# A fused attention and feed-forward block: norm of the fourth block moved to VectorE, output tiles in other banks, a store on another queue, new engine orders

## What is computed

```python
x = x + layernorm(attention(layernorm(x), W_qkv))      # one head of width 128
z = layernorm(x)
h = silu(z @ w1.T * s1) * (z @ w2.T * s2)              # 128 -> 512, gated
h = gelu(h @ h1.T * sh1)                               # 512 -> 512
h = gelu(h @ h2.T * sh2)                               # 512 -> 512
x = x + layernorm(h @ w3.T * s3)                       # 512 -> 128
```

## Time and profile before

| | us |
|---|---|
| median of 3 runs | 134.03 |
| lowest and highest | 133.97 and 134.73 |
| the profiled execution | 134.5 |
| its span, first to last instruction | 132.6 |
| TensorE busy in the span | 125.5 |
| VectorE busy | 104.7 |
| ScalarE busy | 98.5 |
| GpSimd busy | 28.3 |

### The profile page before, as it was taken

One profiled execution on the slowest core, in us unless ns is written; L12 is line 12 of the kernel. 1 busy time (PEld: TensorE's weight loads), 2 busy tenths in 40 slices (PEclk: granted clock), 3 DMA queues, 4 the chain that ended last, 5 costly groups with the idle time before them and its releaser, 6 DMA issues. The chain is left out here.

```text
span 132.6 us, 2374 instructions
## 1 busy us (share of the span) xinstructions
PE 125.5 (95%) x699; PEld 103.3 (78%) x699; DVE 104.7 (79%) x356; ACT 98.5 (74%) x184; POOL 28.3 (21%) x39
## 2 busy tenths in 40 slices
PE   6999998999989999999999999999999999999970
PEld 4685968889876888887889888888776788789960
DVE  1769599999899998938799999566989973996433
ACT  3128779878799919389999277799991996996640
POOL 4281330034210013400200174300002530000352
PEclk9999999999999999999999999999999999999996
DMA  4899997000200000000000001020000002000002
GB/s 112 262 278 405 374 374 240 0 0 5 82 0 5 0 5 2 0 0 0 5 0 0 0 5 40 2 79 7 0 0 0 0 0 84 0 5 0 2 29 94
DMA packets 5344, 8.28 MB, mean 62 GB/s; under 512 B 464, under 2 KB 2768, under 8 KB 5328
## 3 DMA queue, kind: packets, MB, share of 16 engines
q1 hardware_dynamic: 3984, 5.19, 12.3%
q0 software_dynamic: 1344, 2.88, 6.6%
HBM read 7.02 MB, written 1.05 MB: 61 GB/s over the span
## 5 line engine op out<-in xcount | busy, mean ns | idle before, releaser
L317 POOL TENSOR_TENSOR rstd<-ve,minus_half 128x4 f32<-128x4 f32 (+1 forms) x19 | 18.5, 974 | 92.7 <-DVE ve L678 51.6
L1147 PE MATMUL F<-a_hi,h_hi 128*128 128x512 f32 (+1 forms) x160 | 37.7, 357 | 0.0
L1153 PE MATMUL F<-a_lo,h_hi 128*128 128x512 f32 (+1 forms) x160 | 37.3, 353 | 0.1
L610 DVE TENSOR_TENSOR a_lo<-act_full,a_hi 128x512 fp32r<-128x512 f32 (+1 forms) x52 | 30.0, 604 | 3.7 <-ACT act_full L427 3.2
L435 ACT ACTIVATE a_hi<-F,sc 128x512 fp32r<-128x512 f32 (+1 forms) x35 | 21.1, 625 | 14.6 <-PE F L1153 14.5
L1153 PEld LDWEIGHTS F<-a_lo,h_hi 128*128 128x128 f32 x160 | 26.8, 188 | 5.4 <-DVE a_lo L610 1.1
L1147 PEld LDWEIGHTS F<-a_hi,h_hi 128*128 128x128 f32 x160 | 26.0, 188 | 4.5 <-DVE a_hi L716 0.6
L427 ACT ACTIVATE act_full<-F,sc 128x512 f32<-128x512 f32 (+1 forms) x40 | 23.3, 619 | 1.0 <-PE F L1153 1.0
L708 DVE SCALAR_TENSOR_TENSOR act_full<-F,sc,silu 128x512 f32<-128x512 f32 (+1 forms) x16 | 10.7, 681 | 1.7 <-ACT silu L416 1.4
L1104 PE MATMUL F<-x2T_hi,w_hi 128*128 128x512 f32 (+1 forms) x32 | 10.3, 404 | 0.5 <-DVE x2T_lo L610 0.3
L416 ACT ACTIVATE silu<-F,sc 128x512 f32<-128x512 f32 (+1 forms) x16 | 9.8, 634 | 0.9 <-PE F L1107 0.7
(11 more groups left out here) (154 smaller groups left out, 197.5 us busy)
## 6 DMA issues: line engine op xcount, KB each, us to landing
h_raw<-h SPq DMA_DIRECT2D x2, 1024.0 KB, 11.4
h_hi<-h POOLq DMA_DIRECT2D x2, 1024.0 KB, 8.7
xs<-x SPq DMA_DIRECT2D x3, 256.0 KB, 3.7
out<-outs SPq DMA_DIRECT2D x3, 256.0 KB, 2.2
w_raw<-w SPq DMA_DIRECT2D x1, 512.0 KB, 6.6
w_hi<-w POOLq DMA_DIRECT2D x1, 512.0 KB, 7.4
xs<-x SPq DMA_DIRECT2D x2, 128.0 KB, 7.8
w_raw<-w SPq DMA_DIRECT2D x1, 256.0 KB, 15.1
```

Source lines behind the costliest of these rows:

```text
L317: nc.gpsimd.tensor_tensor(rstd[:, ln, tiles(b)], ve[:, ln, tiles(b)], minus_half[:, 0:SIZES[b]], ALU.pow).then_inc(rstd_ready[ln], 1)
L610: nc.vector.tensor_tensor(dst, full, hi.bitcast(f32), ALU.subtract).then_inc(done, 1)
L1147: nc.tensor.matmul(out, terms[k][0], terms[k][2], start=(k == 0), stop=False)
L1153: last = [nc.tensor.matmul(out, terms[k][0], terms[k][3], start=False, stop=(k == KT - 1)) for out, terms in groups]
```

## The change

- `y_normalised(3)` goes from ScalarE to VectorE, right behind `y_shifts(3)`; `last_add(3)` waits for it by a semaphore of its own.
- `last_bank(t)` is F[t] in place of A[2], A[1]: the last tiles' products wait for the last block's gelus, no longer for the fourth block's norm. The eight `last_down` come in another order.
- `store_last(1)` is issued by ScalarE, and `store_last(0)` by SyncE as before.
- `LOW_PARTS` puts w1 and w2 alone in the first group and all else in the second. The first hidden layer's branch asks the second flag, so that `low_sum(5)`, `copy_flags(1)` and `read_flag(1)` come before the end of `A1` of block 0.
- Nine of the twenty high parts of A1 are copied by ScalarE (`HIGH_ON_ACT`). `pT_copy(1, 0)`, `pT_copy(2, 0)` and `gT_copy(3)` go to ScalarE, `xT_copy(2)` and `gT_copy(2)` to VectorE.
- GpSimd issues the rounding loads of w1, w2, h1 and h2 behind its first root. TensorE has one more warm-up product before the first transposes.
- The lists of ScalarE, VectorE, GpSimd and TensorE are rearranged, through all five blocks. `GELU_ONCE` says what `CAST_SLICES` said, and `gated` gives the same buffer.

The diff, cut to the definitions, the orders of the first two blocks and the last, and some of VectorE's between:

```diff
@@ -80,7 +80,7 @@
         ones_sq, w3_diag, w3_row = sb("ones_sq", [P, P]), sb("w3_diag", [P, D]), sb("w3_row", [P, D])
         w3_scaled = sb("w3_scaled", [P, KT * D])
         flags = sb("flags", [1, 2])
-        LOW_PARTS = ((0, 3), (3, 6))
+        LOW_PARTS = ((0, 1), (1, 6))
@@ -182,12 +182,14 @@
-        third_cast = sem("third_layer_cast")
+        a1_hi_by_act = sem("a1_hi_by_act")
+        a_cast = [None] + [sem(f"a{n}_cast") for n in (2, 3)]
...
-        y_shift_ready, yn_ready, out_ready, last_ready, out_stored = (
-            sem("y_shift_ready"), sem("yn_ready"), sem("out_ready"), sem("last_ready"), sem("out_stored"))
+        y_shift_ready, yn_ready, yn_by_dve, out_ready, last_ready, out_stored = (
+            sem("y_shift_ready"), sem("yn_ready"), sem("yn_by_dve"), sem("out_ready"), sem("last_ready"), sem("out_stored"))
+        last_stored = sem("last_stored")
@@ -198,14 +200,19 @@
-        CAST_SLICES = 1
+        HIGH_ON_ACT = (1, 1, 0, 0, 0, 1, 1, 1, 0, 0, 0, 1, 0, 0, 1, 1, 0, 0, 0, 1)
+
+        GELU_ONCE = ((), (12,))
 
         def hi_done(n, b, o):
-            if n < A3 or b < LAST - 1:
-                return a_hi_ready[n], KT * b + o + 1
-            if o < CAST_SLICES:
-                return third_cast, o + 1
-            return a_hi_ready[A3], KT * b + o + 1 - CAST_SLICES
+            i = KT * b + o
+            if n == A1:
+                on_act = HIGH_ON_ACT[i]
+                return (a_hi_ready[A1], a1_hi_by_act)[on_act], sum(e == on_act for e in HIGH_ON_ACT[0:i + 1])
+            by_cast = GELU_ONCE[n - 1]
+            if i in by_cast:
+                return a_cast[n], by_cast.index(i) + 1
+            return a_hi_ready[n], i + 1 - sum(k < i for k in by_cast)
@@ -221,7 +228,7 @@
-        BY_DVE = ((0, 0, 0, 1, 1), (0, 0, 0, 1, 1), (0, 0, 0, 1, 1), (1, 1, 0, 1, 1, 1, 0, 1))
+        BY_DVE = ((0, 0, 1, 1, 1), (0, 0, 1, 0, 1), (0, 0, 0, 1, 1), (1, 0, 0, 0, 1, 1, 0, 1))
@@ -245,7 +252,7 @@
-            return (A[2], A[1], A[3], A[0])[t]
+            return F[t]
@@ -285,8 +292,8 @@
-            store_last(1)
-            sp.wait_ge(out_stored, 16 * (LAST + SIZES[LAST]))
+            sp.wait_ge(out_stored, 16 * (LAST + SIZES[LAST] - 1))
+            sp.wait_ge(last_stored, 16)
@@ -331,29 +338,32 @@
-                pool.wait_ge(yn_ready, T0[b + 1])
+                if b == LAST - 1:
+                    pool.wait_ge(yn_by_dve, SIZES[b])
+                else:
+                    pool.wait_ge(yn_ready, T0[b + 1])
...
             rsqrt(LN_X, 0)
+            round_w12()
+            round_h1()
+            round_h2()
             rsqrt(LN_X, 1)
-            round_w12()
             rsqrt(LN_X, 2)
-            round_h1()
             rsqrt(LN_O, 0)
-            round_h2()
             rsqrt(LN_X1, 0)
+            round_w3()
             rsqrt(LN_O, 1)
             rsqrt(LN_X1, 1)
-            round_w3()
             rsqrt(LN_X, 3)
             rsqrt(LN_O, 2)
             rsqrt(LN_Y, 0)
+            rsqrt(LN_X, 4)
             rsqrt(LN_X1, 2)
-            rsqrt(LN_X, 4)
+            last_add(0)
+            rsqrt(LN_Y, 1)
             rsqrt(LN_O, 3)
-            rsqrt(LN_Y, 1)
-            last_add(0)
@@ -416,6 +426,13 @@
+            def high(n, b, o):
+                c = slice(0, width(b))
+                if b > 0:
+                    act.wait_ge(*a_used(n, b))
+                act.wait_ge(a_full[n], KT * b + o + 1)
+                nc.scalar.activation(a_hi[n][:, o, c], full_of(n, b)[:, o, c], ACT.Copy).then_inc(a1_hi_by_act, 1)
...
+            def store_last(t):
+                g, j = G0[LAST] + t // 2, t % 2
+                act.wait_ge(last_ready, t + 1)
+                nc.scalar.dma_start(out_view[:, g, j * D:(j + 1) * D], outs[:, T0[LAST] + t, :]).then_inc(last_stored, 16)
@@ -467,23 +489,24 @@
             qk_copy()
             xT_copy(0)
             gT_copy(0)
+            exps(0, 0)
             v_copy(0)
-            exps(0, 0)
             xT_copy(1)
             low_sum(0)
             gT_copy(1)
-            xT_copy(2)
             low_sum(1)
+            v_copy(1)
             exps(1, 0)
-            v_copy(1)
-            gT_copy(2)
+            v_copy(2)
             exps(1, 1)
             x2T_high(0)
             silu(0, 0)
+            pT_copy(1, 0)
             silu(0, 1)
-            v_copy(2)
+            pT_copy(1, 1)
+            high(A1, 0, 0)
             silu(0, 2)
-            pT_copy(1, 1)
+            high(A1, 0, 1)
             silu(0, 3)
             exps(2, 0)
             gelu_high(A2, 0, 0)
@@ -491,39 +514,44 @@
             gelu(A2, 0, 0)
             gelu(A2, 0, 1)
             gelu_high(A2, 0, 2)
+            gelu(A2, 0, 2)
             gelu_high(A2, 0, 3)
-            gelu(A2, 0, 2)
             gelu(A2, 0, 3)
+            exps(2, 1)
             gelu_high(A3, 0, 0)
+            x2T_high(1)
+            gelu_high(A3, 0, 1)
             gelu(A3, 0, 0)
-            gelu_high(A3, 0, 1)
+            gelu_high(A3, 0, 2)
             gelu(A3, 0, 1)
-            x2T_high(1)
-            gelu_high(A3, 0, 2)
+            gelu(A3, 0, 2)
+            pT_copy(2, 0)
             gelu_high(A3, 0, 3)
-            gelu(A3, 0, 2)
             gelu(A3, 0, 3)
             silu(1, 0)
             silu(1, 1)
-            exps(2, 1)
             silu(1, 2)
             silu(1, 3)
+            high(A1, 1, 1)
+            high(A1, 1, 2)
             scaled_yT(0)
+            high(A1, 1, 3)
             gelu_high(A2, 1, 0)
@@ -591,9 +623,9 @@
             gelu(A2, 4, 3)
             gelu(A3, 4, 0)
             gelu(A3, 4, 1)
-            y_normalised(3)
             gelu(A3, 4, 2)
             gelu(A3, 4, 3)
+            store_last(1)
...
+            def y_normalised(b):
+                dve.wait_ge(y_shift_ready, b + 1)
+                dve.wait_ge(out_ready, b)
+                for t in range(SIZES[b]):
+                    n = T0[b] + t
+                    nc.vector.tensor_scalar(y_n[:, t, :], A[2][:, t * D:(t + 1) * D], rstd[:, LN_Y, n:n + 1], y_shift[:, n:n + 1],
+                                            ALU.mult, ALU.add).then_inc(yn_by_dve, 1)
@@ -795,35 +835,35 @@
             squared_sums(0)
             w3_row_copy()
             pT_copy(0, 0)
+            xT_copy(2)
             attention_out(0)
             maxima(1, 0)
             x1_block(0)
             maxima(1, 1)
+            copy_flags(0)
+            x1_normalised(0)
             low_sum(2)
-            x1_normalised(0)
-            pT_copy(1, 0)
-            squared_sums(1)
-            copy_flags(0)
+            gT_copy(2)
             x2T_low(0)
             low_sum(3)
             low_sum(4)
             gate(0, 0)
+            low_sum(5)
             gate(0, 1)
-            high(A1, 0, 0)
-            high(A1, 0, 1)
-            low_sum(5)
+            maxima(2, 0)
             low(A1, 0, 0)
             gate(0, 2)
             low(A1, 0, 1)
             high(A1, 0, 2)
-            maxima(2, 0)
+            gate(0, 3)
             low(A1, 0, 2)
+            high(A1, 0, 3)
+            copy_flags(1)
+            squared_sums(1)
+            low(A1, 0, 3)
             attention_out(1)
-            gate(0, 3)
-            copy_flags(1)
-            high(A1, 0, 3)
-            low(A1, 0, 3)
             x1_block(1)
+            maxima(2, 1)
             low(A2, 0, 0)
             low(A2, 0, 1)
             low(A2, 0, 2)
@@ -832,128 +872,119 @@
             x_statistics(3)
             x2T_low(1)
             low(A3, 0, 0)
+            squared_sums(2)
+            x_statistics(4)
+            low(A3, 0, 1)
+            low(A3, 0, 2)
             x_normalised(3)
-            pT_copy(2, 0)
-            maxima(2, 1)
-            low(A3, 0, 1)
+            pT_copy(2, 1)
+            low(A3, 0, 3)
             gate(1, 0)
             gate(1, 1)
             high(A1, 1, 0)
-            high(A1, 1, 1)
-            low(A3, 0, 2)
+            xT_copy(3)
             low(A1, 1, 0)
-            low(A3, 0, 3)
-            pT_copy(2, 1)
+            gate(1, 2)
             low(A1, 1, 1)
-            gate(1, 2)
             gate(1, 3)
-            high(A1, 1, 2)
-            squared_sums(2)
-            high(A1, 1, 3)
             low(A1, 1, 2)
+            attention_out(2)
             low(A1, 1, 3)
-            attention_out(2)
             y_statistics(0)
+            y_shifts(0)
             x1_block(2)
             low(A2, 1, 0)
             low(A2, 1, 1)
             low(A2, 1, 2)
             low(A2, 1, 3)
-            xT_copy(3)
             x1_normalised(2)
-            y_shifts(0)
+            low(A3, 1, 0)
             x2T_low(2)
-            low(A3, 1, 0)
...
+            low(A1, 2, 2)
             gate(2, 3)
-            low(A1, 2, 2)
-            squared_sums(3)
-            high(A1, 2, 3)
+            y_statistics(1)
+            low(A1, 2, 3)
             attention_out(3)
-            low(A1, 2, 3)
-            y_statistics(1)
+            low(A2, 2, 0)
             x1_block(3)
```

(54 more changed lines are left out.)

101 lines of the change are left out of this document (50 added, 51 removed).

## The result

The changed kernel takes 135.47 us (median of 10 runs, 134.79 to 136.25) beside 134.01 for the kernel before (10 runs, 133.46 to 134.73): a ratio of 1.0096, 95% interval [1.0066, 1.0126]. It is 1.3 to 1.5 us slower, where 0.26 less was forecast. The profiled execution took 136.25 us with a span of 134.4, against 134.5 and 132.6 before. Executions more than 1.5 per cent above the fastest of their kernel are left out of all ratios; the traces of e1 and e11 are of such executions.

What follows compares the result with a forecast made beforehand. VectorE and ScalarE were taken to bound the kernel up to about 45 us, TensorE after. Terms of +0.19 to the last products and -0.45 for the tail gave -0.26: 133.8 us from 134.03, 8 in 10 within 132.4 to 135.5.

Steps and rivals of the forecast that it cites:

- blocks 1 to 3, +0.45: Up to 89 us: VectorE waits for two roots, TensorE's products in hand cover nearly all; +0.45 us, between 0 and 1.95.
- The flag: Last weight sum, flag copy and flag read come some 5 us earlier on VectorE, still ready in time; 0.
- The loads, 0: GpSimd's earlier rounding loads cost 0 if the raw h1 weights slip by less than 1.6 us, as assumed.
- The second hidden layer of block 0, +1.16: VectorE idles for GpSimd's root before x1_block(1), so A2's low parts come late; +1.16 us, between 0 and 1.4.
- The stalls at 36.94 and 40.51: TensorE's waits before block 0's later transposes and block 1's A1 go; terms -0.31 and -0.36 us.
- the whole first stretch: First x1 transposes of block 0 to its first y transposes; terms behind the first up give +0.24 us.
- 96 to 112 us, -0.65: Blocks 3 and 4: high parts on ScalarE relieve VectorE, evening TensorE's starts; -0.65 us, between 0 and -0.7.
- The tail, -0.45: From the last products on: norm on VectorE, earlier last gelu, separate store queues; -0.45 us, between -0.1 and -0.6.
- The warm-up, +0.10: A seventh warm-up product on TensorE before the first transposes; +0.10 us, between 0 and +0.21.
- The rival in which the roots reach TensorE: VectorE's waits for GpSimd's roots delay TensorE in every block, no relief at 96 to 112 us; 135.9 us, chance 0.16.
- the three signs that were to show the forecast wrong: ScalarE idle at its second weight sum; second-layer TensorE stall over 0.5 us from block 1; table switch above 1.3.
- the drain: Rival: ScalarE's table switch costs 2.66 us with a 1380 ns drain, delaying x2T_high(1) by 2.8; 136.0 us, chance 0.02.

Runs made afterwards that it cites:

- e1: The changed kernel with GpSimd's rounding loads back at their old places: 135.16 us, 1.0077 of the kernel before.
- e11: e5 with low_sum(5) reading the long-landed raw h2 weights instead of w3, so no wait for w3: 134.22 us, 0.9995 of the kernel before.
- e5: The changed kernel with GpSimd's last_add(0) and last_add(1) waiting until VectorE has written the normalised x1 two blocks on: 134.37 us, 1.0005 of the kernel before.
- e6: e5 with GpSimd's rounding loads also back at their old places: 134.02 us, 0.9990 of the kernel before.
- e10: e6 with squared_sums(1) and attention_out(1) earlier on VectorE, and x1_block(2) ahead of y_shifts(0): 134.86 us, 1.0049 of the kernel before.
- e2: The changed kernel, loads still early, with low_sum(5) moved behind low(A1, 0, 0) on VectorE: 135.19 us, 1.0092 of the kernel before.
- e4: The kernel before with only the tail of the change: 134.01 us, 0.9999 of the kernel before.
- e12: e6 with the tail of the kernel before: 134.34 us, 1.0023 of the kernel before.
- e8: The kernel before with y_shifts(1) moved ahead of xT_copy(4) and low(A2, 2, 2), so an add meets VectorE's norm: 134.65 us, 1.0038 of the kernel before.
- e3: The kernel before with only GpSimd's loads moved early as in the change: 133.80 us, 0.9996 of the kernel before.

## Why the prediction was wrong

**The step that failed most: blocks 1 to 3, +0.45.** It went through VectorE's waits for roots and asked whether TensorE's products in hand cover them. What it left out is that moving `y_shifts` moves three things: the shifts on VectorE, the norm on ScalarE, and the add on GpSimd, and that the last one's cost depends on what VectorE does at that moment. The forecast took VectorE's four instructions at 1.11 us wherever they stand. They measured 1.54 and 2.12; 0.92 us reached TensorE in the trace, and the time fell by 0.91 per cent, 1.2 us with 0.6 of uncertainty, when the adds were held back (e5 against the kernel after). The row that could have warned was in the trace of before: the add ran behind the norm, at 85.20 behind 84.6, by half a microsecond.

Without the collision this stretch costs +0.83 (e6), inside the range of 0 to 1.95 but nearly twice the 0.45. It was not the first root: e10 takes VectorE's wait for it away, and TensorE's stretch stays at 9.0. In e6 one low part of block 1's second layer starts 0.29 later than even, at 49.39; the rest was not traced to a cause.

**The flag, "VectorE had them done ... and now still has", priced at 0.** The place of the sum was checked against TensorE's need, not against the landing of its own data. In the trace this costs 1.14 us (16.59 against 15.45). In the time it is small: 0.19 per cent from e1, 0.15 from e6 against e5, 0.10 from e11, each with an uncertainty of 0.4 to 0.5. Where it didn't wait, the sum came 3.5 to 3.7 us behind the first x1 transposes in the kernels with its new place (e2 apart), and w3 landed between 22.40 and 23.66 in the five traces with early loads. An execution whose transposes start at 20 would hardly wait (20 + 3.6 against 23.66 at the latest); the profiled ones of the kernel after and e5 started at 18.9 and 18.1 and paid it whole.

That most executions simply begin late is unlikely. From the first x1 transposes to the end the trace of e11 takes 113.48 us, and the spans of its eleven shorter executions are 131.5 to 132.7, which puts their transposes at 18.0 to 19.2, an estimate that holds if the part behind them repeats as it does in the traces. The same working gives medians of 18.6 to 19.1 for e1 to e4 and e6 to e12, but 18.2 for the kernel after and 17.9 for e5, the two that were traced with the wait. If these begin like the others, they paid not the whole 1.14 but between 0 and 0.7 of it. Then w3 must land earlier in most executions than in the traces; no trace shows that, and the reason stays open.

**The loads, 0.** The forecast took the raw h1 weights to slip by less than 1.6 us. They slipped by 2.1 (12.39 to 14.53), and ScalarE idled for 0.53. That the term is 0 all the same is luck: ScalarE's next wait, for TensorE, hid it.

**The second hidden layer of block 0, +1.16,** was right in its mechanism: idle of 1.16 for the root, the lows late. Its size was too big: TensorE's low products start 1.14 later than even (1.19 in e6), where 1.6 was forecast; beside the 0.4 that the forecast had for before, this is about +0.75. The stalls at 36.94 and 40.51 are gone, as forecast. Without the wait for w3 the whole first stretch is -0.15 against +0.24 forecast (e6).

**96 to 112 us, -0.65,** was mis-sized. The pair of products that started 0.56 apart in the earlier trace rows does start 0.47 apart after the change, but from y of block 2 to the x1 transposes of block 4 all that is gained is 0.27: 7.97 us instead of 8.24. Of this 0.16 (0.23 in e6) is lost again before the last products. Part of that may be the same as above: GpSimd's third add, beside subtractions with two inputs in memory, takes 1725 ns instead of 1300, and the subtraction at its end 887 instead of 683.

**The tail, -0.45,** measured -0.44 in the trace, with its steps: the last gelu ends 0.67 us behind the start of the last products instead of 1.13, these take 1.95 us instead of 2.12, the last stores are 0.27 apart (less than 0.2 was expected). In the time it can't be told from 0.

**The warm-up, +0.10, and the part ahead of the first x1 transposes** can't be checked: this landmark scatters by more than a microsecond from one trace to the next.

**Rivals and signs.** The rival in which the roots reach TensorE gave 135.9, near the measured 135.5, and 135.5 is also the slow end of the range given for 8 in 10. Both are luck: the time was close and the mechanism was another. Of the three signs that were to show the forecast wrong, one came: ScalarE idles at its second weight sum. It is not what made the kernel slower. No second layer from block 1 on has a stall above 0.5 (the largest is 0.29), and a table switch still takes 1.30 us from its load to the next activation (27.01 to 28.30 in e6), so the drain stays out. The loss sat in the transposes, which the list of signs did not watch.

Summed up: with both unforeseen losses out, the kernel (e6) takes 0.999 of the time before, 133.9 us where 133.77 was forecast; the two make the other 1.4. How near 133.9 is to 133.77 says little, at 0.4 of uncertainty. In the traces e6 is 0.20 us longer than before from the first x1 transposes to the end (113.47 against 113.27), where the terms of this part were to give -0.41: too little gained at 96 to 112 us and too much lost in blocks 1 to 3, in part made up by the second hidden layer.

## What to carry to other kernels

When a step moves, follow every instruction that it releases to its own engine, and for each add on GpSimd ask which instruction of VectorE runs at that time; an add on an engine that has time to spare can hold another engine for nearly the add's own length. Check a moved reader against its writer too: the time at which its data arrive, and how that time and its turn scatter. Where two engines are both full, judge a place in one list by what the other engine waits for, not only by TensorE.

## What the runs showed of the hardware

**GpSimd's add holds up VectorE's norm.** A norm instruction (tensor_scalar, 128x128) of 341 ns that starts just behind the start of an add takes 768 or 1347 ns and ends 90 ns behind it, at 58.05 and 85.69 in the kernel after, and 1320 ns in e8, 84 ns behind it; the length follows the add's end, which looks like a block for the rest of the add and not like a slower rate. The Trainium skill, "SBUF — State Buffer", section "Who interferes with whom", says that the two engines share one pair of ports, which VectorE uses in its 2-port modes, that whoever comes first holds it for its whole instruction, and that the other stands still. The traces agree. Not each instruction suffers: in the kernel before, BATCH_NORM_STATS2 keeps its 276 ns beside the add at 79.07; in e5 the copy from a bank at 85.63, beside the add, took 426 ns, its usual length. By the same section a copy or tensor_scalar can enter these modes, and a tensor_tensor with both inputs in SBUF contends with a GpSimd instruction that reads SBUF, which fits the add of 1725 ns.

**A load's landing depends on another queue's issues.** With GpSimd's first three rounding loads issued 3 to 10 us earlier (4.61, 5.35 and 6.11 in the kernel after, 7.93, 9.70 and 16.14 before) and its last at 18.44 instead of 32.86, SyncE's w3 load landed at 22.4 to 23.7 us in five executions; with them at their old places, at 18.8 to 21.8 in nine. It was issued between 5 and 6.5 us in both. Which part of sharing the DMA engines delays it was not tested.

**The beginning scatters more than the rest.** The first x1 transposes start at 18.1 to 20.0 us in twelve of the fourteen traces and at 20.2 and 20.5 in the other two, although the kernels are nearly the same up to there, while the stretch from there to the last products repeats to within 0.3 us (before, e3, e4: 107.03, 107.02, 107.27; e6, e12: 107.67, 107.70). For a question of half a per cent the traces are to be compared from a landmark behind it.
